# Routed u written back into its PSUM bank and read there, ScalarE's expert numbers loaded two shared tiles sooner

## The reference

```
logits = einsum('ed,btd->bte', gate_w, x); scores = sigmoid(logits) + gate_b
weights, indices = top_k(scores, 4); weights = weights / weights.sum(-1)
shared_out = silu(x @ w1_shared) * (x @ w3_shared) @ w2_shared
h1 = einsum('btd,edc->btec', x, w1_routed)      # c = 176 hidden columns
h2 = einsum('btd,edc->btec', x, w3_routed)
h3 = silu(h1 * h2)
experts_out = einsum('btec,ecd->bted', h3, w2_routed)
routed_out = einsum('bted,bte->btd', experts_out, router_probs)
```

## Time and profile before

| | |
|---|---|
| median of 3 runs | 1235.47 us (1235.09 to 1237.89) |
| profiled execution | 1241.66 us |
| its span in the trace | 1239.6 us |
| mean granted TensorE clock | 0.989 of full speed |
| TensorE busy | 1190.4 us, 96% of the span |
| VectorE busy | 940.1 us, 76% |
| ScalarE busy | 618.3 us, 50% |
| GpSimd busy | 633.1 us, 51% |

### The profile page before, as it was taken

One profiled execution on the slowest core, in us unless ns is written; L12 is line 12 of the kernel. 1 busy time (PEld: TensorE's weight loads), 2 busy tenths in 40 slices (PEclk: granted clock), 3 DMA queues, 4 the chain that ended last, 5 costly groups with the idle time before them and its releaser, 6 DMA issues.

```text
span 1239.6 us, 27512 instructions
## 1 busy us (share of the span) xinstructions
PE 1190.4 (96%) x10106; PEld 1068.9 (86%) x10106; DVE 940.1 (76%) x1849; ACT 618.3 (50%) x1353; POOL 633.1 (51%) x568
## 2 busy tenths in 40 slices
PE   7999999999987899999999999999999999999997
PEld 6788888888776788888789999999999999999996
DVE  5657677777676499999778788887887667777686
ACT  4434443443433466666555455545554555556443
POOL 3022433442445377777477767776664444444442
PEclk9999999999999899999999999999999999999999
DMA  8554623652657133333312101120010000000001
GB/s 254 203 171 171 206 91 134 212 174 72 234 200 310 50 113 112 108 115 112 107 56 65 31 27 61 30 65 27 26 61 1 35 1 1 1 1 1 1 27 43
DMA packets 66722, 114.98 MB, mean 93 GB/s; under 512 B 7968, under 2 KB 36512, under 8 KB 65440
## 3 DMA queue, kind: packets, MB, share of 16 engines
q1 hardware_dynamic: 60448, 96.45, 23.2%
q0 software_dynamic: 6144, 16.79, 4.2%
HBM read 48.85 MB, written 60.16 MB: 88 GB/s over the span
## 4 chain that ended last, share of the span: by engine, by line
PE 81%; issue 6%; POOL 4%; DVE 4%; ACT 2%; another core or an unknown queue 2%; DMA 1%; SPq 0%; ACTq 0%; POOLq 0%; DVEq 0%
PE six L885 7%; PE bank L942 5%; PE bank L940 5%; PE bank L941 5%; PE six L981 5%; PE bank L1018 2%; PE bank L1016 2%; PE bank L1017 2%; PE bank L953 2%; PE bank L952 2%; PE bank L954 2%; PE six L982 2%; POOL cells_scratch L2043 2%; PE six L1005 2%; PE bank L485 2%
## 5 line engine op out<-in xcount | busy, mean ns | idle before, releaser
L2148 POOL TENSOR_TENSOR up_l<-experts,up_h 128x704 fp32r<-128x704 f32 x79 | 134.0, 1697 | 71.3 <-ACT up_h L1295 71.3
L1887 DVE TENSOR_TENSOR sq<-xs 128x512 f32<-128x512 f32 x128 | 131.0, 1024 | 37.5 <-ACT xs L1366 37.5
L2109 POOL TENSOR_TENSOR rstd<-msq,half_pow 128x8 f32<-128x8 f32 x64 | 106.0, 1657 | 95.8 <-DVE msq L1894 94.0
L2121 POOL TENSOR_TENSOR pT<-pT,tri_mul 128x512 f32<-128x512 f32 x64 | 82.0, 1281 | 142.5 <-ACT pT L1395 142.5
L1347 ACT ACTIVATE pT<-six,rstd 128x256 f32<-128x256 f32 x128 | 60.8, 475 | 169.1 <-PE six L982 169.1
L2034 POOL TENSOR_TENSOR hid_l<-hid,hid_h 128x256 fp32r<-128x256 f32 x64 | 50.1, 784 | 147.7 <-ACT hid_h L1118 147.6
L1435 DVE TENSOR_TENSOR yT1l<-six,yT1h 128x512 fp32r<-128x512 f32 x64 | 44.3, 692 | 84.5 <-ACT yT1h L1400 84.5
L940 PE MATMUL bank<-bw_h,xT1h 128*128 128x512 f32 x256 | 105.6, 412 | 0.8 <-ACT v L1371 0.8
L942 PE MATMUL bank<-bw_l,xT1h 128*128 128x512 f32 x256 | 100.3, 392 | 0.0
L941 PE MATMUL bank<-bw_h,xT1l 128*128 128x512 f32 x256 | 99.9, 390 | 0.0
L2112 POOL TENSOR_TENSOR qn<-xs,rstd 128x256 f32<-128x256 f32 x128 | 91.6, 737 | 5.0
(11 more groups left out here) (331 smaller groups left out, 4031.6 us busy)
## 6 DMA issues: line engine op xcount, KB each, us to landing
cells_scratch<-zeros SPq DMA_DIRECT2D x8, 4352.0 KB
xg<-cells_scratch SPq DMA_DIRECT2D x79, 128.0 KB, 2.0
cells_scratch<-y SPq DMA_DIRECT2D x79, 128.0 KB, 1.7
experts<-pack_experts_dram SPq DMA_DIRECT2D x16, 608.0 KB
raw<-pack_attn_dram SPq DMA_DIRECT2D x8, 1024.0 KB
qkA<-qkc SPq DMA_DIRECT2D x64, 64.0 KB, 2.3
w_full<-pack_w_dram SPq DMA_DIRECT2D x4, 512.0 KB, 7.3
out_dram<-x_all SPq DMA_DIRECT2D x8, 256.0 KB, 2.1
```

What stands on the lines that cost most here:

```text
L1887: dve.tensor_tensor(out=sq[:, tt, :], in0=x_qk, in1=x_qk, op=ALU.mult).then_inc(sq_sb, 1)
L2109: pool.tensor_tensor(out=rstd[:, r, :], in0=msq[:, r, :], in1=half_pow[:], op=ALU.pow).then_inc(rstd_sb, 1)
L2148: pool.tensor_tensor(out=up_l[:, r, :], in0=weights(expert_of(i), 0, UW), in1=up_h[:, r, :].bitcast(F32), op=ALU.subtract).then_inc(up_lo, 1)
```

## The change

In the routed tiles VectorE writes u over h1 in the PSUM bank rather than in SBUF. ScalarE's tanh and VectorE's z read it there. Since the bank is now read until z is made, TensorE's `expert_up` two tiles later waits for z (`z2_sb`) where it waited for u (`u2_sb`), and z waits for the write of u (`u2_sb`) as well as for the tanh. Apart from that, ScalarE reads the experts' numbers into its registers before the tanh of shared tile 14 (`NS - 2`), not after the last shared tile.

```
 def expert_up(m, i, r):                      # TensorE
-    pe.wait_ge(u2_sb, m - 1)
+    pe.wait_ge(z2_sb, m - 1)
...
 def expert_tanh(m, r):                       # ScalarE
     act.wait_ge(u2_sb, m + 1)
-    act.activation(th2[:, r, :], u2[:, r, :], ACT.Tanh, scale=0.5).then_inc(th2_sb, 1)
+    act.activation(th2[:, r, :], banks[r][:, 0:HE], ACT.Tanh, scale=0.5).then_inc(th2_sb, 1)
...
 for m in range(NS):                          # ScalarE, shared tiles
...
+    if m == NS - 2:
+        act.wait_ge(tables_made, 1)
+        expert_of = experts_of_tiles(mybir.EngineType.Activation)
     shared_tanh(m)
...
-act.wait_ge(tables_made, 1)
-expert_of = experts_of_tiles(mybir.EngineType.Activation)
 act.wait_ge(experts_loaded, 16 * NE)
...
 def expert_hidden(m, r):                     # VectorE
     dve.wait_ge(h2_sb, m - NS + 1)
-    dve.tensor_tensor(out=u2[:, r, :], in0=banks[r][:, 0:HE], in1=h2[:, r, :], op=ALU.mult).then_inc(u2_sb, 1)
+    dve.tensor_tensor(out=banks[r][:, 0:HE], in0=banks[r][:, 0:HE], in1=h2[:, r, :], op=ALU.mult).then_inc(u2_sb, 1)

 def expert_silu(m, r):                       # VectorE
     dve.wait_ge(th2_sb, m + 1)
+    dve.wait_ge(u2_sb, m + 1)
     dve.wait_ge(z2_ps, m - 1)
-    dve.scalar_tensor_tensor(out=z2[:, r, 0:HE], in0=th2[:, r, :], scalar=1.0, in1=u2[:, r, :],
+    dve.scalar_tensor_tensor(out=z2[:, r, 0:HE], in0=th2[:, r, :], scalar=1.0, in1=banks[r][:, 0:HE],
                              op0=ALU.add, op1=ALU.mult).then_inc(z2_sb, 1)
```

## The result

The changed kernel takes 1229.53 us in the median of 5 runs (1225.12 to 1229.94), against 1235.55 for the kernel before (1235.09 to 1238.73, 5 runs). The ratio is 0.9933 with a 95% interval of 0.9911 to 0.9955, that is 5.6 to 11.0 us less; the prediction said 8.7 less, and 1226.8. The profiled execution took 1229.64 us, 12.0 less than the profiled execution of before; its span is 1227.5, 12.1 less.

What follows compares the result with a forecast made beforehand. TensorE was taken to bound the kernel at 2.275 us per routed tile, the rest being waits for z. 7.1 + 0.4 + 1.3 - 0.1 = 8.7 us less than 1235.47 gave 1226.8 us, range 1222.5 to 1232.0.

Steps and rivals of the forecast that it cites:

- What bounds the kernel: Routed tiles: TensorE needs 2.275 us per tile, the length of the turn without a wait; the rest is waiting for z.
- z in PSUM: Routed tiles: z reading u from PSUM is no longer held beside up_l and takes 0.34 us, bounds 0.28 to 1.07.
- u written to PSUM: Routed tiles: VectorE's u written to the bank takes 0.33 us as before, bounds 0.28 to 1.44.
- The slack of 0.7 us: Routed tiles: what is left of VectorE's turn, 1.56 of 2.275 us being used, hides a longer u.
- the dear write: Rival, chance 0.04: writing u in place is slow, a loss from 0.81 us more for u; total 1258 us.
- th from PSUM, the two waits: Routed tiles: tanh reading PSUM is worth nothing; expert_up waiting for z, and z for u's write, are free.
- The sum over the tiles: Routed tiles 1 to 73: 72 turns fall from 2.373 to 2.275 us each, 7.1 us less.
- the last five turns: End of the routed tiles, with pieces of the next weights: 0.4 us gained, bounds nothing to 1.0.
- The table's load: ScalarE's load of the experts' numbers, moved ahead of shared tile 14's tanh, saves 1.29 us before the first up_h.
- the cost to the shared tiles: The load at its new place delays tile 14's tanh by up to 0.9 us; counted as 0.1, bounds 0 to 0.9.
- the rival that it does not fall at all: Rival, chance 0.30: the clock holds through the gap before the first expert_up, 2.8 us more gained, 1224.0 us.
- The range: Total time: 1225.5 (tail gain 1.0, no delay) to 1229; down to 1222.5 with clock held, up to 1232.0, turns stopping halfway.

Runs made afterwards that it cites:

- small up_l: Kernel before, both z inputs in SBUF, GpSimd making only 8 of 704 up_l columns from the third routed tile on: 1232.82 us, ratio to before 0.9917.
- the one with four copies: Changed kernel with four extra 176-column copies out of the bank on VectorE ahead of each routed z: 1257.95 us, ratio to before 1.0124.
- the th experiment: Changed kernel, but th instead of u goes through the PSUM bank and u stays in SBUF: 1231.75 us, ratio to before 0.9918.
- two copies: Changed kernel with two extra 176-column copies out of the bank on VectorE ahead of each routed z: 1229.57 us, ratio to before 0.9906.
- The two repeats: Changed kernel run again unaltered, twice, beside the kernel before: 1232.05 us against 1240.89, and 1228.43 us against 1237.04.
- four other profiles: Changed kernel with two copies, with fill matmuls after rows_T, with the first up_h sooner, and that also filled: 1229.57, 1230.65, 1226.64, 1226.09 us.

## Why the prediction was right

*What bounds the kernel.* Right. The short turn without a wait was TensorE's own: 2.277 to 2.279 us in every kernel that freed z, whether by u in PSUM, by th in PSUM or by a small up_l, but for the one with four copies, where VectorE is the bound.

*z in PSUM.* Right, 0.33 us against 0.34 taken. That the block needs both inputs in SBUF was inferred from xTl; the th experiment shows it directly, and the small up_l shows the other half.

*u written to PSUM.* u became 22 ns longer, 8 of them for the write and the rest because it now starts after a pause. The write is not held by GpSimd either. The slack of 0.7 us that I set against it is real: two copies (0.48 us) vanish in it, four do not. The prediction put the threshold of the dear write at 0.81 us; the copies only bracket it, with no loss at 0.48 us and 14.7 us lost at 0.98. The price that the rival needed is not there.

*th from PSUM, the two waits.* Free, as said. L875 waits for nothing in the stretch, and no wait of L864 for z appears.

*The sum over the tiles.* 7.1 predicted, 6.95 measured; for the last five turns 0.4 and 0.41. The gain there did not grow because bw_l took over part of the wait. Before, z had taken the wait and the four bw_l of these turns took 0.68 us each; now they take 1.23, 0.87, 0.82 and 1.13. With the small up_l they take 0.68 to 0.69, and the five turns 11.37.

*The table's load.* 1.29 predicted, 1.40 measured; the cost to the shared tiles was put at 0.1 and is nothing that the trace shows: the tanh of tile 14 came 0.58 us later, rows_T did not. Mis-sized is what came with it: the sum held that the low clock lasts as before, and the rival that it does not fall at all. It fell, for half as long, which is worth 1.0 us; where it held, in four other profiles, 1.6 us more were gained there, so 2.6 in all for the rival's 2.8. With the 1.0 the places of the change give 9.7 us (1.40 + 0.98 + 6.95 + 0.41), 1.0 more than the sum.

*The forecast of 1226.8* missed the first median by 2.7 us, within the scatter of the runs. The two repeats, 8.8 and 8.6 us less, bear out the difference of 8.7. That they meet it to 0.1 is luck: their intervals are some 2 us to either side, and the sum had left out 1.0 us of clock.

*The range* was not worked out cleanly. A tail gain of 1.0 in place of 0.4 and no delay take the 1226.8 to 1226.1, not 1225.5, and with the clock held to 1223.3, not 1222.5; turns that stop halfway give about 1230.4, not 1232.0. The measured 1229.5 lies within either.

## What to carry to other kernels

When two engines are both nearly full, look for the turn that has no wait in it: its length is the bound that is left, and the difference times the count is the gain. An instruction whose duration spreads from 0.33 to 1.44 us for the same shape was here not slow but held. It ended at a fixed distance from what held it, and one of its two inputs moved from SBUF to PSUM freed it. The next instruction in the queue with two inputs in SBUF (bw_l) inherited part of the wait, so look for others of the form.

## What the runs showed of the hardware that I had not expected

- VectorE writing its result over its own PSUM input took 350 ns for 176 columns, 342 with the output in SBUF, both after a pause of VectorE. With the output in SBUF and no pause ahead of it it took 328.
- A VectorE instruction of 0.68 us (bw_l) that started 0.09 or 0.15 us after a GpSimd instruction of 1.7 us took 2.16 and 2.09 us, ending 0.55 us after it; z, of 0.33 us, ended 0.18 to 0.21 after. So about 0.13 us of the held instruction's own time passes while it stands. GpSimd's instruction is 1.70 us with and without it.
- The stretch of low clock after a gap of 1.86 us came in six of seven profiles with this gap and not in the seventh (the two copies). In three of the four profiles without it (all but the two copies) the clock fell after the routed tiles, which made the rest 1.4 to 1.7 us longer than the 631.0 to 631.2 of the others. The kernel with four copies had both, so the one does not exclude the other. Whether the one brings the other about was not tried.
